# Five of sixteen tiles of exponentials summed by accumulating DMAs, nine by GpSimd additions, three denominator groups

## The reference

```
scores = einsum('bhqd,bhkd->bhqk', q, k) / sqrt(32)
attn   = softmax(scores, axis=-1)
out    = einsum('bhqk,bhkd->bhqd', attn, v)
```

## Time and profile before

| what | value |
|---|---|
| median of 3 executions | 3634.0 us (3624.8 to 3634.88) |
| the profiled execution | 3630.94 us, its span 3629.3 us |
| mean granted clock of TensorE | 0.925 of full speed |
| attention phase | about 415 to 2510 us of the span |
| unit without routing steps (head 3) | 56.5 us between the stores of the maxima |
| the other units of a chunk | 65.0, 63.6 and 70.9 us |

### The profile page before, as it was taken

The page is one execution under the profiler, slowest core; times in us unless marked ns, Lnnn a source line. Parts: engine busy times, 40 slices in busy tenths (PEclk is TensorE's granted clock), DMA queues, the critical chain, the costliest instruction groups (busy, mean ns, idle before and its releaser), DMA issues. The chain is left out here.

```text
span 3629.3 us, 55108 instructions
## 1 busy us (share of the span) xinstructions
PE 3177.5 (88%) x16936; PEld 2057.7 (57%) x16936; DVE 2186.3 (60%) x3738; ACT 1618.3 (45%) x3252; POOL 2015.1 (56%) x912
## 2 busy tenths in 40 slices
PE   5878799999998999999999999983999999999900
PEld 4666444454444554454554544533999999999900
DVE  5776878778677777777786787722233333332235
ACT  2332165556455555555555565552333333433311
POOL 2342189879789789889888798892000000000064
PEclk7998699999999999999999999996999999999955
DMA  3443625121211213112121121003222122222066
GB/s 104 163 148 141 174 79 157 34 53 39 57 36 46 53 33 77 22 44 66 22 62 47 39 49 41 13 14 122 70 91 90 69 92 69 88 82 82 27 237 211
DMA packets 199285, 285.39 MB, mean 79 GB/s; under 512 B 86295, under 2 KB 91415, under 8 KB 196485
## 3 DMA queue, kind: packets, MB, share of 16 engines
q1 hardware_dynamic: 176720, 221.11, 21.5%
q0 software_dynamic: 16640, 51.77, 3.9%
q10 hardware_dynamic: 5685, 9.49, 0.7%
HBM read 169.17 MB, written 115.41 MB: 78 GB/s over the span
## 5 line engine op out<-in xcount | busy, mean ns | idle before, releaser
L1140 DVE TENSOR_REDUCE p_mxp<-p_ps_a 128x1 f32<-128x512 f32 x2048 | 1283.7, 682 | 312.4 <-PE p_ps_a L1316 300.1
L1060 ACT ACTIVATE p_PR<-p_ps_b 128x512 f32<-128x512 f32 x2048 | 1067.4, 602 | 838.1 <-PE p_ps_b L1330 792.4
L931 POOL TENSOR_TENSOR p_PP<-p_PP,p_PR 128x2048 f32<-128x2048 f32 x224 | 1026.8, 4584 | 32.8 <-ACT p_PR L1060 16.5
L1316 PE MATMUL p_ps_a<-p_KS,p_QS 96*128 96x512 f32 x2048 | 845.1, 444 | 43.5 <-DMA p_KS<-kh_d 16.8
L1330 PE MATMUL p_ps_b<-p_QS,p_KS 98*128 98x512 f32 x2048 | 753.0, 414 | 8.5 <-ACT p_PR L1060 7.5
L927 POOL TENSOR_TENSOR p_PP<-p_PR 128x2048 f32<-128x2048 f32 x128 | 586.3, 4581 | 289.4 <-ACT p_PR L1060 227.4
L1316 PEld LDWEIGHTS p_ps_a<-p_KS,p_QS 96*128 96x128 f32 x2048 | 395.0, 196 | 492.9 <-DVE p_mxp L1140 249.1
L1336 PE MATMUL p_ps_pv<-p_PR,p_VS 128*32 128x512 f32 x4096 | 533.1, 619 | 67.7 <-ACT p_PR L1060 54.3
L1569 POOL DMA_DIRECT2D ye_d<-p_YE x80 | 43.5, 543 | 899.0 <-DVE p_YE L1678 899.0
L1330 PEld LDWEIGHTS p_ps_b<-p_QS,p_KS 98*128 98x128 f32 x2048 | 394.3, 193 | 189.5 <-ACT p_PR L1060 98.8
L1614 ACT ACTIVATE p_hf<-p_ps_h 128x384 f32<-128x384 f32 (+1 forms) x256 | 112.2, 438 | 559.2 <-PE p_ps_h L83 553.8
(11 more groups left out here) (169 smaller groups left out, 3406.7 us busy)
## 6 DMA issues: line engine op xcount, KB each, us to landing
p_w_raw<-in_L_ffn_w SPq DMA_DIRECT2D x16, 2048.0 KB, 9.3
xe_d<-p_SR SPq DMA_DIRECT2D x20, 1024.0 KB, 9.3
ye_d<-p_YE POOLq DMA_DIRECT2D x80, 256.0 KB, 2.3
p_QS<-qh_d SPq DMA_DIRECT2D x64, 256.0 KB, 3.9
p_KS<-kh_d SPq DMA_DIRECT2D x64, 256.0 KB, 6.3
p_XE<-xe_d SPq DMA_DIRECT2D x16, 768.0 KB, 7.3
p_X<-in_x SPq DMA_DIRECT2D x8, 1024.0 KB, 7.4
x_d<-p_x SPq DMA_DIRECT2D x8, 1024.0 KB, 4.4
```

The costliest lines, as they stand in the source:

```text
L931: nc.gpsimd.tensor_tensor(PP[:, buf, :, :], PP[:, buf, :, :], PR[:, PR_AT[tile], :, :], ALU.add).then_inc(add_made, 1)
L1060: nc.scalar.activation(PR[:, PR_AT[kt], j, :], ps_b[:, B_AT[n], :], ACT.Exp, scale=SCALE).then_inc(ex_made, 1)
L1140: nc.vector.reduce_max(mxp[:, a // (S // CH), a % (S // CH):a % (S // CH) + 1], ps_a[:, bank, :], AXX).then_inc(a_read, 1)
L1316: nc.tensor.matmul(ps_a[:, bank, :], QS[0:96, g, j, t * P:(t + 1) * P], KS[0:96, g, kb * CH:(kb + 1) * CH], start=True, stop=True).then_in ...
```

## The change

Of a unit's 16 tiles five (5, 7, 9, 11, 13) are now summed by DMA. When tile 5's exponentials are done, ACT issues a plain DMA that copies them into a new buffer `PD` (`copy_tile`). When tile 7's are done, and the copy has landed, GpSimd issues a DMA that adds them into `PD` (`send_tile`, `accum_op`), and so on for 9, 11 and 13, each after the one before has landed. Of the other eleven tiles two groups are left to GpSimd's additions, (0,1,2,3,4,6) and (8,10,12,14,15): nine additions. There are three denominator groups: two D stand at the head of tile 4 for the unit before (`D_LATE` 2), one in tile 12; those of tiles 11, 13 and 15 are gone. An issue of `send_tile` stands in GpSimd's queue behind the last addition that needs an earlier tile: sends 7 and 9 behind the addition of tile 6, send 11 behind that of tile 10, send 13 behind that of tile 12. ACT waits for the copy or the DMA where a buffer's old tile was one of the five. The numbers of `RANK_AT`, `FINISH_AT` and `SENDS` are given anew for nine additions.

```diff
--- before.py
+++ after.py
@@ -645,22 +645,24 @@
 
 
 
-    BASE = ["VABBABAB", "AVABAABBAB", "AVABABBAB", "VABBBAABA", "DABBABAAB", "ABBAVVBAB", "BAABBABV", "VAABABBAB",
-            "VABAABBAB", "VVAABABBAB", "VAABBABABAV", "DABABBAAB", "ADABBAABB", "ABADABABAB", "ABBABABAVVVM", "BABBAABAD"]
+    BASE = ["VABBABAB", "AVABAABBAB", "AVABABBAB", "VABBBAABA", "DDABBABAAB", "ABBAVVBAB", "BAABBABV", "VAABABBAB",
+            "VABAABBAB", "VVAABABBAB", "VAABBABABAV", "ABABBAAB", "ADABBAABB", "ABAABABAB", "ABBABABAVVVM", "BABBAABA"]
     EXTRA = {0: {11: "O", 13: "O", 15: "O"}, 1: {1: "O", 10: "R", 11: "R", 12: "R", 13: "R"}, 2: {0: "L", 8: "K"}, 3: {}}
     ORDER = [[BASE[kt] + EXTRA[g].get(kt, "") for kt in range(KT)] for g in range(KV)]
-    TURN, V_LATE, D_LATE = 13, 2, 1
-
-    GROUPS = [(0, 1, 2, 3), (4, 5, 6, 7), (8,), (9, 10, 11, 12), (13, 14, 15)]
+    TURN, V_LATE, D_LATE = 13, 2, 2
+
+
+    GROUPS = [(0, 1, 2, 3, 4, 6), (5, 7, 9, 11, 13), (8, 10, 12, 14, 15)]
+    BY_DMA = 1
     PR_AT = [0, 1, 2, 3, 4, 0, 1, 2, 3, 4, 0, 1, 2, 3, 4, 5]
 
     INVERT_AT, ATT_AT, LOW_AT = {4: (0,), 5: (1,), 6: (2,), 7: (3,)}, 8, 9
     SQUARES_AT = {(0, 12): 0, (0, 14): 1, (1, 0): 2, (1, 2): 3}
     POWER_AT, NORM_AT, SCALE_AT = (1, 2), {(1, 1): (0, 1), (1, 3): (2, 3)}, {(1, 8): (0, 1), (1, 9): (2, 3)}
 
-    WEIGH_AT, RANK_AT, FINISH_AT = (2, 2), (2, 5), (2, 8)
+    WEIGH_AT, RANK_AT, FINISH_AT = (2, 2), (2, 4), (2, 6)
     EXP_AT, INVERT_1_AT, INVERT_2_AT, SUM_AT = 1, 3, 7, 12
-    SENDS = {(3, 0): (0,), (3, 1): (1,), (3, 2): (2,), (3, 4): (3,), (3, 5): (4,), (3, 6): (5,), (3, 7): (6,), (3, 9): (7,)}
+    SENDS = {(3, 0): (0,), (3, 1): (1,), (3, 2): (2,), (3, 3): (3,), (3, 4): (4, 5), (3, 5): (6,), (3, 6): (7,)}
 
     AK, BK = 3, 3
     NA = G * TT * (S // CH)
@@ -675,10 +677,16 @@
     EARLY = NA - A_AT[TURN]
     assert A_AT[KT] == NA and all("M" not in o for o in BASE[:TURN])
     NS = len(GROUPS)
-    ADDS = sorted((tiles[k], n, k) for n, tiles in enumerate(GROUPS) for k in range(1, len(tiles)))
-    MULTI = [n for n, tiles in enumerate(GROUPS) if len(tiles) > 1]
+    ADDS = sorted((tiles[k], n, k) for n, tiles in enumerate(GROUPS) for k in range(1, len(tiles)) if n != BY_DMA)
+    MULTI = [n for n in range(NS) if n != BY_DMA]
+    SENT_TILES = GROUPS[BY_DMA]
+    NT = len(SENT_TILES) - 1
+
+    SEND_TILE = {}
+    for k, tile in list(enumerate(SENT_TILES))[1:]:
+        SEND_TILE.setdefault(max(n for n, add in enumerate(ADDS) if add[0] < tile), []).append(k)
     GROUP_OF = {t: n for n, tiles in enumerate(GROUPS) for t in tiles}
-    assert len(MULTI) % 2 == 0 and sum("".join(BASE).count(x) for x in "D") == NS
+    assert len(MULTI) == 2 and sum("".join(BASE).count(x) for x in "D") == NS
 
     def added(tile):
 
@@ -750,6 +758,7 @@
         VS = s.sb("VS", [P, KV, KT, HD])
         PR = s.sb("PR", [P, 6, G, CH])
         PP = s.sb("PP", [P, 2, G, CH])
+        PD = s.sb("PD", [P, G, CH])
         mxp = s.sb("mxp", [P, TT * G, S // CH])
         mxv = s.sb("mxv", [P, TT, G])
         mh = s.sb("mh", [G, CH], F32R)
@@ -797,7 +806,7 @@
         y_in, ss_made, sv_made, rstd_made, normed, sr_made = (s.sem(n) for n in ("y_in", "ss_made", "sv_made", "rstd_made", "normed", "sr_made"))
         lgt_made, route, sel_made, exp_made, inv_made, placed, summed = (s.sem(n) for n in ("lgt_made", "route", "sel_made", "exp_made", "inv_made", "placed", "summed"))
         src_st, slot_st, wt_st, sent, gate_sem = (s.sem(n) for n in ("src_st", "slot_st", "wt_st", "sent", "gate"))
-        dve_const, inverted = s.sem("dve_const"), s.sem("inverted")
+        dve_const, inverted, tile_copied, tile_sent = (s.sem(n) for n in ("dve_const", "inverted", "tile_copied", "tile_sent"))
         block = s.block()
 
         def gate(eng):
@@ -915,20 +924,28 @@
             def add(u, n, first):
 
                 tile, group, k = ADDS[n]
-                buf = MULTI.index(group) % 2
+                buf = MULTI.index(group)
                 if k == 1:
 
-                    m = MULTI.index(group)
-                    if m >= 2:
-                        pool.wait_ge(den_mm, NS * u + MULTI[m - 2] + 1)
-                    elif not first:
-                        pool.wait_ge(den_mm, NS * (u - 1) + MULTI[m - 2] + 1)
+                    if not first:
+                        pool.wait_ge(den_mm, NS * (u - 1) + group + 1)
                     pool.wait_ge(ex_made, NSC * u + G * (tile + 1))
-                    nc.gpsimd.tensor_tensor(PP[:, buf, :, :], PR[:, PR_AT[tile - 1], :, :], PR[:, PR_AT[tile], :, :], ALU.add).then_inc(add_made, 1)
+                    nc.gpsimd.tensor_tensor(PP[:, buf, :, :], PR[:, PR_AT[GROUPS[group][0]], :, :], PR[:, PR_AT[tile], :, :], ALU.add).then_inc(add_made, 1)
                 else:
                     pool.wait_ge(ex_made, NSC * u + G * (tile + 1))
                     pool.wait_ge(add_made, len(ADDS) * u + n)
                     nc.gpsimd.tensor_tensor(PP[:, buf, :, :], PP[:, buf, :, :], PR[:, PR_AT[tile], :, :], ALU.add).then_inc(add_made, 1)
+
+            def send_tile(u, k):
+
+                if k == 1:
+                    pool.wait_ge(tile_copied, 16 * (u + 1))
+                else:
+                    pool.wait_ge(tile_sent, 16 * (NT * u + k - 1))
+                pool.wait_ge(ex_made, NSC * u + G * (SENT_TILES[k] + 1))
+                gate(pool)
+                pool.dma_start(PD[:].rearrange("p g q -> p (g q)"), PR[:, PR_AT[SENT_TILES[k]], :, :].rearrange("p g q -> p (g q)"),
+                               accum_op=ALU.add).then_inc(tile_sent, 16)
 
             def norm_power(c):
 
@@ -1008,6 +1025,8 @@
                 for g in range(KV):
                     for n in range(len(ADDS)):
                         add(unit(c, g), n, first and g == 0)
+                        for k in SEND_TILE.get(n, ()):
+                            send_tile(unit(c, g), k)
                         if first:
                             continue
                         if (g, n) == POWER_AT:
@@ -1051,13 +1070,22 @@
                     if kt >= back or not first:
                         old, at = (kt - back) % KT, u if kt >= back else u - 1
                         act.wait_ge(pv_mm, KT * at + old + 1)
-                        if len(GROUPS[GROUP_OF[old]]) > 1:
+                        if old in SENT_TILES:
+                            k = SENT_TILES.index(old)
+                            act.wait_ge(tile_copied if k == 0 else tile_sent, 16 * (at + 1) if k == 0 else 16 * (NT * at + k))
+                        else:
                             act.wait_ge(add_made, len(ADDS) * at + added(old))
-                        else:
-                            act.wait_ge(den_mm, NS * at + GROUP_OF[old] + 1)
                 n = NSC * g + G * kt + j
                 act.wait_ge(sc_mm, NB * c + n + 1)
                 nc.scalar.activation(PR[:, PR_AT[kt], j, :], ps_b[:, B_AT[n], :], ACT.Exp, scale=SCALE).then_inc(ex_made, 1)
+
+            def copy_tile(u, first):
+
+                if not first:
+                    act.wait_ge(den_mm, NS * (u - 1) + BY_DMA + 1)
+                act.wait_ge(ex_made, NSC * u + G * (SENT_TILES[0] + 1))
+                gate(act)
+                act.dma_start(PD[:].rearrange("p g q -> p (g q)"), PR[:, PR_AT[SENT_TILES[0]], :, :].rearrange("p g q -> p (g q)")).then_inc(tile_copied, 16)
 
             def values_out(u, first=False):
 
@@ -1105,6 +1133,8 @@
                                     values_out(unit(c, g), first and g == 1)
                             if what == "O" and not first:
                                 projected.append(slot_of(c, g, kt, pos)[0] + 1)
+                        if kt == SENT_TILES[0]:
+                            copy_tile(unit(c, g), first and g == 0)
                         if kt == ATT_AT and not (first and g == 0):
                             high(unit(c, g) - 1, (g - 1) % KV)
                         if (g, kt) in SQUARES_AT and not first:
@@ -1340,12 +1370,12 @@
             def denominators(u, n):
 
                 tiles = GROUPS[n]
-                if len(tiles) > 1:
+                if n == BY_DMA:
+                    pe.wait_ge(tile_sent, 16 * NT * (u + 1))
+                    src = PD
+                else:
                     pe.wait_ge(add_made, len(ADDS) * u + added(tiles[-1]))
-                    src = PP[:, MULTI.index(n) % 2, :, :]
-                else:
-                    pe.wait_ge(ex_made, NSC * u + G * (tiles[0] + 1))
-                    src = PR[:, PR_AT[tiles[0]], :, :]
+                    src = PP[:, MULTI.index(n), :, :]
                 for j in range(G):
                     last = nc.tensor.matmul(ps_den[HD * j:HD * (j + 1), :], ones[:, 0:HD], src[:, j, :],
                                             start=(n == 0), stop=(n == NS - 1))
```

## The result

The changed kernel takes 3747.4 us (median of 4, 3740.8 to 3752.0); the kernel before took 3629.4 us beside it. The ratio is 1.033 (95% interval 1.030 to 1.035): 118 us slower, where 3600 us, a gain, was forecast, and above the range's 3665. The profiled execution has a span of 3750.4 us.

What follows compares the result with a forecast made beforehand. PE was taken as the bound, busy 88% of the span. 25 ordinary units x 1.27 us (32 us) plus 7 head-3 units x 0.6 (4 us) give 36 us less: 3598, rounded to 3600 us; range 3570 to 3665.

Steps and rivals of the forecast that it cites:

- L: Time of an accumulating 1 MB DMA from issue to semaphore: taken as 6.6 us, bounds 4.1 and 10.9.
- the low end: Lower bound of the accumulating DMA's time: the second read costs nothing, 1.65 + 2.46 = 4.1 us.
- the chain: GpSimd's sends, each waiting for the one before: free in ordinary units up to a landing time of about 10.7 us.
- Denominator matmuls: PE, each unit: five groups become three, net 1.97 us saved; tile 13's removal gives back 0.3 us (bounds 0 and 1.0).
- ACT's issue: ACT's queue, between exps of tiles 5 and 6: the copy's issue costs 0.2 us per unit, bounds 0 and 0.5.
- 1.97 us gross: PE's saving per unit from fewer denominator groups, before deductions: 63 us in 32 units.
- The maxima's transfer: Start of the next unit, with send 13 possibly still moving: 0.2 us per ordinary unit, bounds 0 and 1.5.
- Head 3: GpSimd's queue before exp 13: exp 13 about 1 us later than before; such a unit gains 0.6 us instead of 1.97.
- The clock: PE's clock: part of its dips behind longer stalls in head 3, covered by rounding 3598 to 3600.
- Rival 1: Slower: the accumulation chain sets the unit, L over 9.4 us; 3666 us at L 10.0, 3820 at 12; chance 0.27.
- Its two sums: Rival 1 at L = 10: 77 us lost against 42 gained, 3666 us; at L = 12: +190 us, 3820.

Runs made afterwards that it cites:

- f4: Changed kernel with GpSimd's fourth DMA (tile 13) as a plain copy instead of an accumulating one: 3695.1 us in one execution.
- f3: Kernel before without the denominator group of tile 8 in tile 13 and without ACT's wait for it: 3621.3 us, ratio 0.997.
- e4: Changed kernel with SP instead of ACT issuing the copy of tile 5, at the same point: 3725.4 us, ratio 1.028.
- e2: Changed kernel with send 13 behind the addition of tile 14 instead of that of tile 12: 3660.4 us, ratio 1.008.
- g2: Kernel before plus one accumulating 1 MB DMA a unit into an unread buffer, issued by GpSimd after tile 14's exponentials: 3701.5 us, ratio 1.0205.
- e3: Changed kernel with head 3's sends of rows moved, none between send 9 and the addition of tile 10: 3684.2 us, ratio 1.015.
- f2: Changed kernel with SP issuing the copy, send 13 behind tile 14's addition, head 3's sends of rows moved, one V moved from tile 14 to 13: 3608.5 us.
- g1: f2 with send 13 behind tile 12's addition again, GpSimd first waiting until the maxima's two transfers have landed: 3651.4 us, ratio 1.007.
- e1: Changed kernel without the four accumulating DMAs and all waits for them: 3610.4 us, ratio 0.995.

## Why the prediction was wrong, step by step

- **L, the accumulating DMA**: 7.1 us for 6.6, inside the bounds. The half microsecond is in the fixed part: the plain send of f4 lands after 4.7 us, where the low end had 4.1. Right, and so was its consequence that ordinary units don't feel the chain: in head 1 no entry but tile 4's, 6's, 11's and those behind tile 12 moves.
- **Denominator matmuls**: the groups of tiles 4, 11 and 15 cost 0.88, 0.85 and 0.8 us, as counted. The one of tile 13 was priced at 1.0 less 0.3 us; it is worth 0 in a unit's table, and f3 shows the same where this group alone (it sums tile 8 and stands in tile 13) is taken out of the kernel before: 0 in an ordinary unit, given back in the same stretch. The bound had been "the whole group", and the row with 11 us of unbroken DVE work stood there; the choice within the bounds was wrong.
- **ACT's issue**: 0.2 us with a bound of 0.5, measured 0.93 (e4). The DMA instruction takes 0.47 us, as its row had it. But it can go only when ACT's own exps are written, so ACT's queue stands until then: the exps of tile 6 begin 0.8 us after the last of tile 5 ended, and the B that needs the first of them goes 0.69 us late. The prediction took the instruction's time for the bound and left out the empty engine on either side of it. With this, 1.97 us gross became 0.
- **The maxima's transfer**: priced at 0.2 us with a bound of 1.5; where it meets send 13 it is 3 to 4 us of stall, 7 where the loop turns, plus the clock. This is the step that failed most: 87 us (e2). Some 19 of them lie in the first chunk, which the prediction charged nothing. The 0.2 went by rows with one queue at a time; none showed two. In the records of the changed kernel send 13 has eight rows per engine, 5.1 us, and the small packets mostly stand behind seven or all of them; accumulating or plain, they do so (f4, g2). The Trainium skill, "DMA: Bandwidth & Descriptors" (Queues, rings and completion order), has an engine take turns between its queues at packet boundaries, where a packet is typically 9 to 17 descriptors (orders to copy one piece, here one row). The prediction, and the rival of g2, took one row for a packet and so came to a wait of a row or two, about 1 us, with which this case's records disagree; that step is theirs and not the page's. If an engine's eight rows were one such packet, the wait for all of them would follow; but at seven ends small packets went in between the rows, so no run here shows where a packet ends.
- **Head 3**: its method, walking GpSimd's queue in order against the times of the exps, found the right place, exp 13, and the right sign; it gave 1 us later than before, where exp 13 comes 4.0 us later and ACT's wait is 4.88. Send 7 goes 27.8 us after the first addition, as it said; send 9 follows 7.8 us behind (it had 6.7), and the addition 8+10 starts 3.6 us behind that (it had 0.7), since two sends of rows with their waits stand between. Worth 63 us with its consequences (e3).
- **The clock**: mentioned as "dips behind longer stalls" and given the 2 us between 3598 and 3600. It is up to 48.
- **Rival 1** named GpSimd standing in its waits, but tied it to L over 9.4 us. The slower side came at L = 7.1, by a queue that the prediction had bounded instead of making it a rival of its own. Its two sums also set different gains against the loss, 42 us at L = 10 and 54 at L = 12 (25 x 5 + 7 x 17 less 190); nothing measured hangs on that. That the time fell outside the range on the slow side, with L inside its bounds, is not this rival come true.

What stays open: how much of f2's gain would be left with an order in which neither send 13, nor the loads, nor the sends of rows meet the maxima, and what in the DMA engines decides after how many rows the small transfer gets its turn (a transfer with many more than eight rows per engine wasn't tried).

## What to carry to other kernels

Before any large transfer is added, whoever issues it, look up each transfer of a few KB on which the bound engine waits: put the large issue where the small one can't fall behind it, or it can cost nearly its whole length. An instruction that is moved or added between others on an in-order queue is priced by the walk of that queue with every DMA, send and wait in it, and a wait added to it costs what stands behind it (g1). Before a removed matmul is booked as gain, look whether another engine works without a gap across that stretch; such a stretch is worth more for hiding work than for removing it (f2 against f3).

## What the runs showed of the hardware

- An accumulating DMA of 128 rows of 8 KB within SBUF: 7.1 us from issue to landing, 0.64 us a row and engine, against 0.32 us plain; its issue takes GpSimd 0.88 us, against 0.58 for a plain one of the same size (f4), which lands after 4.7 us. The instructions beside this traffic hardly changed: GpSimd's additions take 4.61 to 4.65 us on average for 4.58, DVE's maxima 0.68 us as before.
- Small transfers wait for a 1 MB transfer that was issued ahead of them on another queue: at the ends of head 2, where nothing else stands before them, by 2.4 to 4.0 us (6.0 to 7.6 for 3.6). With a send of rows behind it the wait is up to 5.9 us (9.5 for 3.6). The small packets don't always come last: at 7 of 19 late ends some went in between the rows.
- A DMA issue in ACT's queue between two dependent exps takes 0.47 us and keeps ACT from exps for 0.82 us; the same copy issued by SP costs the unit nothing (e4).
- In the changed kernel each stall of PE of 2.3 us and more from 450 to 2400 us (21 of them) is followed or overlapped by a stretch of 3.4 to 14 us at 1.2 GHz. Six of its other seven such stretches begin with no idle time of PE over 0.5 us in the 9 us before. From 450 to 2400 us there are 13 of them in the kernel before (109 us), 28 in the changed one (205), 18 in e2 (123), 22 in e3 (147), 27 in e4 (232), 16 in f2 (113) and 13 in e1 (92).
